# Three fp32r passes for the last batch's value products, and other places in GpSimd's queue for its bias sums, in a transformer block on one core

## The reference, cut to what matters

```python
x = x + 0.5 * ffn(layernorm(x))            # out = sum_k w_k * x @ W[ids_k].T, plus sum_k w_k * b[ids_k]
# attention-like stage on x1 = layernorm(x): k, v, r products of mixes of a token and the one before it,
#   a scan over the tokens (wkv), rwkv = sigmoid(r) * wkv, then x1 + rwkv @ Wo.T = xa
h = layernorm(xa); xk, xr = mixes of h with the token before
kk = relu(xk @ Wck.T) ** 2                 # 1024 hidden channels
kv = kk @ Wcv.T                            # the "values": 1024 -> 256 channels
x = x + xa + sigmoid(xr @ Wcr.T) * kv
x = x + 0.5 * ffn(layernorm(x))            # same adapter weights as in the first line
```

## Time and profile before

| | |
|---|---|
| Median of 3 runs | 431.5 us (431.36 to 431.73) |
| The profiled execution | 431.73 us |
| Its span in the trace | 429.9 us |
| TensorE busy | 417.1 us, 97% of the span |
| VectorE busy | 367.9 us, 86% |
| ScalarE busy | 329.7 us, 77% |
| GpSimd busy | 185.6 us, 43% |
| Granted TensorE clock | 9 tenths or more in every slice of the span; mean 1.00 |

### The profile page before, as it was taken

The page is one execution under the profiler, slowest core; times in us unless marked ns, Lnnn a source line. Parts: engine busy times, 40 slices in busy tenths (PEclk is TensorE's granted clock), DMA queues, the critical chain, the costliest instruction groups (busy, mean ns, idle before and its releaser), DMA issues.

```text
span 429.9 us, 6308 instructions
## 1 busy us (share of the span) xinstructions
PE 417.1 (97%) x2042; PEld 337.0 (78%) x2042; DVE 367.9 (86%) x725; ACT 329.7 (77%) x669; POOL 185.6 (43%) x194
## 2 busy tenths in 40 slices
PE   8989989889999999999999999999999999999996
PEld 8865875568868887798769886888779876988985
DVE  2988989998989999998989998999999898886235
ACT  1157977899799969997899979997999489945420
POOL 1446052727272635635372728263553347033011
PEclk9999999999999999999999999999999999999999
DMA  6992010001000110002000200010000000000101
GB/s 200 376 398 81 2 49 0 0 2 52 0 0 2 57 44 0 0 26 74 2 0 25 74 1 2 0 50 1 2 0 25 26 0 2 25 26 0 50 2 50
DMA packets 15972, 18.52 MB, mean 43 GB/s; under 512 B 1083, under 2 KB 13635, under 8 KB 15939
## 3 DMA queue, kind: packets, MB, share of 16 engines
q1 hardware_dynamic: 14538, 17.05, 11.4%
q10 hardware_dynamic: 1400, 1.07, 0.8%
HBM read 13.92 MB, written 4.19 MB: 42 GB/s over the span
## 4 chain that ended last, share of the span: by engine, by line
PE 77%; DVE 1%; issue 0%; ACT 0%; DVEq 0%
PE pair L484 22%; PE pair L362 10%; PE pair L374 10%; PE pair L458 6%; PE pair L459 6%; PE pair L462 6%; PE pair L352 6%; PE pair L343 4%; PE pair L499 3%; PE pair L428 1%; PE pair L432 1%; PE pair L429 1%; PE pair L514 0%; DVE rwkv L1054 0%; DVE work L1048 0%
## 5 line engine op out<-in xcount | busy, mean ns | idle before, releaser
L484 PE MATMUL pair<-wcv_sb,kk 128*128 128x256 f32 x448 | 100.4, 380 | 0.0
L484 PEld LDWEIGHTS pair<-wcv_sb,kk 128*128 128x128 f32 x448 | 83.8, 190 | 11.3 <-ACT kk L741 0.7
L458 PE MATMUL pair<-xck_hi,wck_hi 128*128 128x512 f32 x128 | 54.4, 425 | 0.0
L462 PE MATMUL pair<-xck_lo,wck_hi 128*128 128x512 f32 x128 | 50.7, 396 | 0.0
L459 PE MATMUL pair<-xck_hi,wck_lo 128*128 128x512 f32 x128 | 50.6, 395 | 0.0
L737 ACT ACTIVATE kk<-pair 128x512 f32<-128x512 f32 x64 | 36.3, 589 | 14.2 <-PE pair L462 13.3
L1349 POOL TENSOR_TENSOR x2b<-xs,bias_bc 128x512 f32<-128x512 f32 (+1 forms) x16 | 21.8, 1364 | 56.6 <-DVE xcr_lo L1127 22.9
L1349 POOL TENSOR_TENSOR x<-x,bias_bc 128x512 f32<-128x512 f32 x14 | 18.1, 1296 | 55.7 <-DVE rwkv L1054 36.3
L741 ACT ACTIVATE kk<-kk 128x512 f32<-128x512 f32 x64 | 35.9, 625 | 0.0
L1389 POOL TENSOR_TENSOR xs<-x,xa 128x512 f32<-128x512 f32 x16 | 20.4, 1273 | 31.6 <-DVE xa L1060 31.0
L1309 POOL TENSOR_TENSOR rstd_x<-vare_x,nhalf 128x4 f32<-128x4 f32 (+2 forms) x26 | 27.3, 1050 | 9.1 <-DVE vare_x L909 7.8
(11 more groups left out here) (173 smaller groups left out, 1119.3 us busy)
## 6 DMA issues: line engine op xcount, KB each, us to landing
x<-in_x_dram SPq DMA_DIRECT2D x8, 512.0 KB, 4.0
out_dram<-xs SPq DMA_DIRECT2D x15, 256.0 KB, 2.1
xt<-in_xt_dram SPq DMA_DIRECT2D x4, 512.0 KB, 8.2
work<-in_ffn_w_dram ACTq DMA_DIRECT2D x4, 256.0 KB, 5.1
work<-in_ffn_w_dram SPq DMA_DIRECT2D x4, 256.0 KB, 5.2
kk<-in_wck_dram SPq DMA_DIRECT2D x1, 1024.0 KB, 9.6
xs<-in_xt_dram SPq DMA_DIRECT2D x2, 512.0 KB, 10.8
wcv_sb<-in_wcv_dram SPq DMA_DIRECT2D x1, 1024.0 KB, 12.5
```

Of the source, the lines that this page charges most:

```text
L458: nc.tensor.matmul(key_bank(n), wck_hi[:, h, cols], xck_hi[:, h, :], start=h == 0, stop=False)
L462: last = nc.tensor.matmul(key_bank(n), wck_hi[:, h, cols], xck_lo[:, h, :], start=False, stop=h == CH - 1)
L484: last = nc.tensor.matmul(bank_of("kv", e, i)[:, t % TB * C:(t % TB + 1) * C], kk[:, n, tok:tok + P], wcv_sb[:, n, :], start=n == 0, stop= ...
```

## The change

TensorE's `last_values` reads kk and the weights Wcv of batch 7 in two fp32r parts each, in three matmuls where there was one. ACT makes `kk_hi` (Square with an fp32r output) ahead of each square of batch 7, in a new order of that batch, and the weights' high part in loop pass e = 6. DVE makes the low parts. The tiles lie in places that are free by then: `kk_hi` over y1s of batches 2 to 5, `wcv_hi` over two of the x1 tiles, the low parts over `kk` and `wcv_sb` themselves. GpSimd's bias sums get other places in its queue and other waits: `bias_to_x2(e-1, 1)` after `xcr_lo`, `bias_to_x2(e, 0)` at the end of the pass after `xcr`, and both `bias_to_x` after the denominators.

```diff
@@ tiles and semaphores
+        kk_hi, kk_lo = in_place_of(f"y1s_{EARLY[0]}", "kk_hi", [P, HB, T]), in_place_of("kk", "kk_lo", [P, HB, T])
+        wcv_hi = [in_place_of(f"x1_{b % X1}", f"wcv_hi_{i}", [P, HB // 2, C]) for i, b in enumerate((LAST - 2, LAST - 1))]
+        wcv_lo = in_place_of("wcv_sb", "wcv_lo", [P, HB, C])
+        kk_hi_done, kk_lo_done, s_wcv_hi, s_wcv_lo = (sem(n) for n in ("kk_hi_done", "kk_lo_done", "s_wcv_hi", "s_wcv_lo"))
@@ TensorE, last_values
+                if t == 0 and 0 in part:
+                    pe.wait_ge(s_wcv_lo, 1)
                 for n in part:
+                    high = wcv_hi[n // (HB // 2)][:, n % (HB // 2), :]
                     if t == 0:
-                        pe.wait_ge(sq_done, HB * LAST + n + 1)
-                    last = nc.tensor.matmul(by_tiles(last_bank(LAST_KV, j), j)[:, t - LAST_PARTS[j][0], :], kk[:, n, t * P:(t + 1) * P], wcv_sb[:, n, :],
-                                            start=n == 0, stop=n == HB - 1)
+                        pe.wait_ge(kk_hi_done, n + 1)
+                    nc.tensor.matmul(dst, kk_hi[:, n, tok], high, start=n == 0, stop=False)
+                    nc.tensor.matmul(dst, kk_hi[:, n, tok], wcv_lo[:, n, :], start=False, stop=False)
+                    if t == 0:
+                        pe.wait_ge(kk_lo_done, n + 1)
+                    last = nc.tensor.matmul(dst, kk_lo[:, n, tok], high, start=False, stop=n == HB - 1)
@@ ScalarE
+            def last_key_parts(n):
+                act.wait_ge(relu_done, HB * LAST + n + 1)
+                nc.scalar.activation(kk_hi[:, n, :], kk[:, n, :], ACT.Square).then_inc(kk_hi_done, 1)
+                key_square(LAST, n)
+            def last_weight_high():
+                act.wait_ge(s_wcv, 1)
+                act.wait_ge(xs_done, BANKS * LAST)
+                for i in range(2):
+                    last = nc.scalar.activation(wcv_hi[i][:, :, :], wcv_sb[:, i * HB // 2:(i + 1) * HB // 2, :], ACT.Copy)
+                last.then_inc(s_wcv_hi, 1)
@@ ScalarE, loop pass e: after relu 0 to 3 and x2t_of(e - 1)
+                if e == LAST:
+                    break
                 key_square(e, 0)
@@ behind squares_x1 and stats_x
+                if e == LAST - 1:
+                    last_weight_high()
@@ behind the loop
+            key_relu(LAST, 4)
+            for n in range(HB - 5):
+                last_key_parts(n)
+                key_relu(LAST, n + 5)
+            for n in range(HB - 5, HB):
+                last_key_parts(n)
+            channel_gate(LAST)
@@ VectorE
+            def last_weight_rest():
+                dve.wait_ge(s_wcv_hi, 1)
+                for i in range(2):
+                    some = slice(i * HB // 2, (i + 1) * HB // 2)
+                    last = nc.vector.tensor_tensor(wcv_lo[:, some, :], wcv_sb[:, some, :], wcv_hi[i][:, :, :].bitcast(F32), ALU.subtract)
+                last.then_inc(s_wcv_lo, 1)
+            def last_key_rest(n):
+                dve.wait_ge(kk_hi_done, n + 1)
+                dve.wait_ge(sq_done, HB * LAST + n + 1)
+                nc.vector.tensor_tensor(kk_lo[:, n, :], kk[:, n, :], kk_hi[:, n, :].bitcast(F32), ALU.subtract).then_inc(kk_lo_done, 1)
@@ VectorE, loop pass e = LAST
-                elif has(e - 1):
+                else:
                     second_rest(e - 1)
+                    last_weight_rest()
+                    for n in range(HB // 2):
+                        last_key_rest(n)
                 if has(e - 1):
                     add_second(e - 1, 0)
...
                 if e == LAST:
+                    for n in range(HB // 2, HB):
+                        last_key_rest(n)
                     break
@@ GpSimd, loop pass e
                 if has(e - 1):
+                    pool.wait_ge(xcr_lo_done, 2 * e + 2)
                     bias_to_x2(e - 1, 1)
                 if e - 1 >= SUMS_X2:
                     inverse_std("x2", e - 1)
-                if has(e - 1):
-                    pool.wait_ge(xcr_lo_done, 2 * e + 2)
-                    bias_to_x2(e - 1, 0)
                 if has(f):
                     mix_r(f)
                     hold_exponents(f)
...
                 if has(f + 1):
-                    pool.wait_ge(aa_done, 2 * f + 2)
+                    pool.wait_ge(den_done, 2 * f + 2)
                     bias_to_x(f + 1, 0)
-                    pool.wait_ge(rwkv_done, 2 * f + 2)
                     bias_to_x(f + 1, 1)
...
                 if has(f + 2):
                     inverse_x(f + 2)
+                if has(f):
+                    pool.wait_ge(xcr_done, 2 * f + 2)
+                    bias_to_x2(e, 0)
```

More of the change, by code:

```diff
@@ L142, in build @@
         kk = sb("kk", [P, HB, T])
+        kk_hi, kk_lo = in_place_of(f"y1s_{EARLY[0]}", "kk_hi", [P, HB, T]), in_place_of("kk", "kk_lo", [P, HB, T])
+        wcv_hi = [in_place_of(f"x1_{b % X1}", f"wcv_hi_{i}", [P, HB // 2, C]) for i, b in enumerate((LAST - 2, LAST - 1))]
+        wcv_lo = in_place_of("wcv_sb", "wcv_lo", [P, HB, C])
+        assert HB // 2 * C == NT * C and HB * T == (B - 4) * NT * C
         wck_raw = kk[:, 0:CH * HID // T, :].rearrange("p n t -> p (n t)").rearrange("p (h o) -> p h o", h=CH)
@@ L495, in last_values @@
                     take(p, i, kvs_done, 2 * LAST + j + 1)
+                dst = by_tiles(last_bank(LAST_KV, j), j)[:, t - LAST_PARTS[j][0], :]
+                tok = slice(t * P, (t + 1) * P)
+                if t == 0 and 0 in part:
+                    pe.wait_ge(s_wcv_lo, 1)
                 for n in part:
+                    high = wcv_hi[n // (HB // 2)][:, n % (HB // 2), :]
                     if t == 0:
-                        pe.wait_ge(sq_done, HB * LAST + n + 1)
-                    last = nc.tensor.matmul(by_tiles(last_bank(LAST_KV, j), j)[:, t - LAST_PARTS[j][0], :], kk[:, n, t * P:(t + 1) * P], wcv_sb[:, n, :],
-                                            start=n == 0, stop=n == HB - 1)
+                        pe.wait_ge(kk_hi_done, n + 1)
[4 more added lines that the diff above has]
+                    last = nc.tensor.matmul(dst, kk_lo[:, n, tok], high, start=False, stop=n == HB - 1)
                 if t == LAST_PARTS[j][-1] and HB - 1 in part:
@@ L1430, in _ @@
                 if has(f + 1):
-                    pool.wait_ge(aa_done, 2 * f + 2)
+                    pool.wait_ge(den_done, 2 * f + 2)
                     bias_to_x(f + 1, 0)
-                    pool.wait_ge(rwkv_done, 2 * f + 2)
                     bias_to_x(f + 1, 1)
-                if has(f + 1):
                     lower("x1", f + 1 - SUMS_X1, x1_done, 2 * (f + 1) + 2)
```

## The result

The changed kernel takes 433.1 us (median of 9 executions, 432.72 to 435.47), the kernel before, measured with it, 431.65 us (9, 431.28 to 432.06). The ratio is 1.0044, 95% interval 1.0025 to 1.0064: slower by 1.45 us where 2.4 us less were forecast. The profiled execution took 433.23 us with a span of 431.1 us.

The account below looks back on a forecast made before the run. TensorE, 97% busy and without waits from 95.3 to 423.7 us, was taken as the bound. Values -2.58, turn +0.32 and line 1033 -0.14 sum to -2.40 us: median 431.5 to 429.1 us, range 428.4 to 430.7.

Parts of the forecast that it names:

- I take 0, nearest to line 1012: DVE's line 1025 scans beside GpSimd's moved `bias_to_x` sums: no delay, within bounds of 0 and 2.1 us a batch.
- Rival A: Line 1025 scans and GpSimd sums exclude each other, delaying `rwkv`; 432.7 us at s = 1.28, 437.6 at 2.1; chance 0.12.
- The sign that I had set for it: In the changed profile, the two line 1025 scans together 1.1 us longer would show the prediction wrong.
- Rival A's price: For DVE delay s per batch: batch 1 pays s - 0.14, batches 2 to 6 each s - 0.82 once s is larger.
- the lead: Batches 2 to 6: `rwkv` ready at 326.66, TensorE reaching it at 327.33, so 0.67 us to spare.
- The values on TensorE: Last batch: 96 fp32r matmuls at 0.1173 us replace 32 float32 at 0.432, -2.58 us; -2.26 after the turn's 0.32.
- The turn's wait: `last_turn(0)` in the last batch still waits for DVE's sum of part 0, giving back 0.32 us.
- The parts in time: Batch 7's high and low parts from ACT and DVE arrive before TensorE needs them, lead 1.3 us at block 7; cost 0.
- The two conditions per block: TensorE's two waits per value block instead of one cost 0, within bounds of 0 and 1.2 us.
- `bias_to_x2`, zero: Moving these GpSimd sums frees DVE's `xk` mixes of 1.06 us, but none of it reaches the kernel's time.
- the wait that I named: DVE's wait, two steps after the `xk` mixes, for ACT's copy of a turned tile timed by TensorE; absorbs 1.06 us.
- Line 1033's relief: With no sum beside it, DVE's line 1033 drops from 1.44 to 1.28 us for two; -0.14 us in batch 1 only.

Follow-up runs that it names:

- scalar_sums: The changed kernel with a one-input GpSimd tensor_scalar instead of the two-input sum in both `bias_to_x` of batches 2 to 7 (bias omitted): 429.8 us, ratio 0.9957.
- one_sum: The changed kernel with only the first `bias_to_x` beside the scans, the second waiting for `rwkv` again: 433.33 us, ratio 1.0053.
- psum_scan: The changed kernel with the scans of aa reading v from PSUM instead of ev from SBUF: 429.66 us, ratio 0.9957.
- split5: The changed kernel with both `bias_to_x` at their old waits and the last batch's first turn behind five blocks of tile 2, not four: 429.68 us, ratio 0.9947.
- x2_only: The kernel before with only the new places of `bias_to_x2`: 431.69 us, ratio 0.9993.
- behind_scan: `split5` with the first `bias_to_x` released by the first of the two scans instead of the second: 429.14 us, ratio 0.9948.
- x_only: The kernel before with only the new waits of `bias_to_x`: 435.61 us, ratio 1.0095.
- filled: The changed kernel with idle matmuls on TensorE ahead of the output product, 8 in batch 1 and 2 in batches 2 to 6: 433.57 us, ratio 1.0048.

## Why the prediction was wrong, point by point

- **The failed step is "I take 0, nearest to line 1012".** The scans beside the sums cost s = 3.39 - 2.33 = 1.06 us a batch, half of the upper bound that stood beside it. Rival A, at 0.12, was what happened. The sign that I had set for it, scans 1.1 us longer, was itself 0.04 us too high. The row that should have decided was the mixes' +1.06 us: the same GpSimd instruction and two SBUF operands. I went by line 1012, where GpSimd's instruction has one operand in SBUF and not two. `scalar_sums` shows that this matters (0.37 us).
- The page SBUF — State Buffer of the Trainium skill (Who interferes with whom) has the rule that decided. `one_sum` and `psum_scan` agree with it in both halves: the second to start waits (2.15 us for a 1.3 us sum, 1.06 us for the scan), and a DVE instruction with one SBUF operand is spared (1.20 us a scan). For GpSimd instructions with one operand it holds on one side only: in `scalar_sums` scan 0 holds the instruction (2.34 us against 1.51), but DVE is not fully blocked by it, neither in line 1012 (0.02 us) nor there (0.37 us for two scans).
- **Rival A's price was undersized.** For s = 1.06 its formula gave 0.92 in batch 1 and 0.24 in each of five, 2.1 us, and with the value passes' -2.26 a time of 431.4 us, no change. So even the right s would have missed the slowdown. Measured are 0.94 and 0.53, 3.6 us. Batch 1 was right. For the others the lead was wrong: I set `rwkv` at 326.66 against 327.33, the chain's piece, where TensorE's record of the output product starts at 327.16. Of these 0.50 us about 0.05 go as well, for a product that waits starts that much behind `rwkv`'s end (in the changed profile 0.05 in each of the six). The lead was 0.45 us and not 0.67. 1.06 - 0.15 - 0.45 = 0.46, measured 0.43; another 0.10 us is the load of the first `rwkv` tile, no longer hidden under the matmul before it (3.56 against 3.45).
- **The values on TensorE**, -2.58 + 0.32 = -2.26: right, measured -2.19. The pace of line 362 held (0.1173 us forecast, 0.118 seen). It is not the 0.109 us that the prediction took from the page TensorE: Matmul & The Clock Gate of the Trainium skill (Back-to-back issue gap), where the formula is given for an isolated matmul. The turn's wait is real, as `split5` gives 0.34 us back.
- **The parts in time:** right. ACT's squares and DVE's low parts never hold TensorE between blocks; the last low part ends at 412.54 us and TensorE's matmul on it starts at 413.70, a lead of 1.2 us where 1.3 were forecast. The two conditions per block are free.
- **`bias_to_x2`, zero:** right, `x2_only` 0.9993 with 1 inside the interval, and the freed 1.06 us vanishes at the wait that I named.
- **Line 1033's relief:** right in size (1.44 to 1.28 us), but it comes with the scans' loss. `behind_scan` has it without.
- **A term I did not have:** executions take 2.1 to 2.2 us more than their span in the kernels with the value passes and 1.8 us in those without (`x_only`, `x2_only` and before). 0.3 us of the gain goes outside of the span. The cause was not looked for and stays open; the value passes also bring four more semaphores and 32 more matmul records.

## What to carry to other kernels

Where GpSimd and DVE both read SBUF, look at each pair of instructions by their operands: two SBUF operands on DVE and two on GpSimd take turns, and a row of that very pair outweighs one of a similar pair. A sum may still start beside such an instruction if it is the last one of its kind in DVE's row. Measure the lead over a full engine from start to start of its records, since the last record before a wait runs on into it, and price a wait that falls in every batch by the period and not by the idle time shown.

## What was not expected of the hardware

The 1.8 us wait of batch 1 may cost more than itself. In the profiled execution of `one_sum`, 435.22 us, the stretch behind the wait was at half the clock, 1.2 GHz, and the output product took 5.41 us instead of 3.72; the period took 48.59 us instead of 46.89. Busy times by stretch (us, then the engines' busy time, the granted clock, DMA):

```profile
80.00:96.40 16.40, 13.91 (x64) 9.63 (x63) 16.40 (x22) 15.20 (x26) 5.83 (x4) 1.00 0.00 0
96.50:99.90 3.40, 3.40 (x9) 2.69 (x9) 2.30 (x9) 2.94 (x8) 1.41 (x2) 0.50 0.00 0
```

```profile
96.21 5.41 PE L358 MATMUL pair<-wo_sb,rwkv 128*128 128x256 f32 x16 [1.79 <-DVE rwkv L1092]
```

Four of the ten executions of `one_sum` took 435.2 us or more, with a mean clock of 0.990 to 0.994, and two of the nine of the changed kernel (435.46 and 435.47, both 0.994); the others lie between 432.7 and 433.6. `x_only`, with the same wait, has two of six (437.47 and 437.24, at 0.996 and 0.995, against a median of 435.61). In the page TensorE: Matmul & The Clock Gate of the Trainium skill (Part 1) activity releases the throttle and idleness brings it back; this stretch, which follows a wait, agrees. But the kernel before, with a wait of 0.9 us there, has such executions too (433.97 us at 0.994), the profiled one of `split5` has its half-clock stretch at 26.8 to 30.2 us and none behind the wait, and `filled` still had one of 7. Counted as executions over 1.5 us above their kernel's median, there are 8 of 25 with the 1.8 us wait and 4 of 59 of the kernel before. So the longer wait very likely makes them more frequent; where the clock fell is seen in one of the eight only, and no run isolates the wait as the cause.
